# Transformer layer on eight cores: abs-sum tile loads alternate between the SyncE and GpSimd queues, some of these sums move into the V projection, and half of the layer-norm evacuations move to VectorE

## Chip, cores and metric

One Trainium2 chip, all eight cores. The time is the device time of one execution in microseconds (us), of the slowest core. Cores 0 to 3 are one die, 4 to 7 the other. Each core works alone on half of the query rows of one of four batch entries; the cores exchange nothing.

## What is computed

The layer is attention and a ternary-quantized FFN, each between layer norms and with a residual. Cut to what matters:

```python
def attn(x, Wq, Wk, Wv, Wo):              # x (4, 2048, 2048), 16 heads of 128
    scores = einsum('bthd,bshd->bhts', q, k) * tril(ones(T, T))
    attn = softmax(scores / T ** 0.5, axis=-1)
    return einsum('bhts,bshd->bthd', attn, v).reshape(B, T, D) @ Wo

def ternary_quant(w):                      # W_up, W_gate (8192, 2048), W_down (2048, 8192)
    scale = mean(abs(w)) + 1e-8
    q = clip(round(w / scale), -1, 1) * scale
    return w + stop_gradient(q - w)

x = x + layernorm(attn(layernorm(x), Wq, Wk, Wv, Wo))
x = x + layernorm(ffn(layernorm(x), W_up, W_gate, W_down))   # silu(up) * gate, down
```

The mask multiplies the scores (masked ones are 0, not minus infinity). What the change is about is `mean(abs(w))`: each core reads all of W_up, W_gate and W_down once, 192 MB in 192 tiles of 128 x 2048 f32 (1 MB each), and sums absolute values, before the FFN can start. The tiles are spread over the attention.

## The kernel before

The program is recorded engine by engine (`sec`, `Rec`) and replayed at one line, L1584 (`_replay`), so every instruction of the trace has this line: tiles tell them apart. Each engine runs its own list in order. `Buf.rd` and `Buf.wr` put the semaphore waits: a reader waits for the last writers of a buffer, a writer also for its readers, and so does a DMA that fills it. A DMA's wait is on the queue of the engine that issues it, so what stands behind it in that engine's list waits as well. SyncE (SP) and GpSimd (POOL) issue all DMAs.

The stages in order. (1) `emit_ln1`, 24 tiles of 128 rows: a load in two halves (`load_xtile`: first half from SP, second from POOL, which waits for the first), statistics (BN_STATS x4 and BN_AGGR) on DVE, rstd and the normalize on ACT, 16 transposes of 128x128 on PE in four groups of four, and one evacuation of 128x512 for each group, all on ACT (`emit_transposes`, default `evac="scalar"`). Three buffers rotate: xtA, xtB, xtC. Groups alternate between two PSUM tiles, psTr and psTr2, so group 2 needs group 0 evacuated. (2) The Q projection, 16 column blocks; the weights of a block are two halves, cast to bf16 on the way, from POOL, in two pairs of buffers (wqkA/wqkB, wqkC/wqkD). (3) Eight groups of two heads. `emit_group`: K of two heads, V of both (16 steps `st`, each 16 matmuls and one DVE cast into Vg), a matmul with U_b and a DVE cast into vsufT, the load of the next group's V weights (`load_wvg`: 16 DMAs on POOL into wvg, "arena_d<-WvR"), then `emit_head` twice. (4) Wo, residual and second layer norm, the FFN, the last layer norm: not touched.

`emit_head` has 16 chunks of shrinking width (1024 down to 128 columns). For a chunk: a score matmul on PE, two chunks ahead ("arena_c,arena_d"); a mask product on DVE in PSUM ("R<-R,arena_d"); the exponential on ACT (into stripA or stripB); on PE the denominator ("ones") and the product with V. At the end DVE adds the counts (den_f), ACT takes Ln and Exp of den_f, POOL stores it (den_spill), DVE casts the head's output (arena_b).

`emit_abs(n, which)` puts the next n abs-sums at the place where it is called. Each is a load of 1 MB into xtA or xtB by turns (both named arena_x in the trace), from SP, and one instruction: Down tiles ("DownR", "act") an Abs with an accumulated sum on ACT, Up and Gate tiles ("UpL", "GateL", by turns, "dve") a TENSOR_REDUCE on DVE into absP. A load waits until the sum before it in its buffer is done. The calls: two after each Q block and two after each K head (`which="any"`: Down tiles first), and one at every second chunk of each head (`which="dve"`), eight in a head. That is 64 Down tiles in the projections, 128 Up and Gate tiles in 16 heads. When "dve" has none left, it takes Down tiles while there are some. In the text the eight of a head are j0 to j7, xtA is A, xtB is B; heads count from 0, groups from 0, and group g has heads 2g and 2g+1.

Of the kernel before, what the change touches and what calls it, by code (L numbers as in the profile page):

```python
# [170 lines left out]
def build_program(p: Par, debug=False):  # L171
# [215 lines left out]
    def next_qreg():  # L387
        r = qkv8[qkv_rr[0] % 8]
        qkv_rr[0] += 1
        return r  # L390
# [7 lines left out]
    def qof(buf, tag):  # L398
        key = (id(buf), tag)
        if key not in dma_ctrs:  # L400
            dma_ctrs[key] = Counter(nc, f"q{tag}.{len(dma_ctrs)}", 16)
        return dma_ctrs[key]
# [27 lines left out]
    with nc.Block() as blk:  # L430

        def sec(engname):
            def runner(fn):
                fn(recs[engname], W[engname])
            return runner

        def dma_in(engname, dst, dst_ap, src_ap, deps=(), tag="i"):
            q = qof(dst, tag)
            @sec(engname)
            def _(e, w):  # L440
                w.wait(*deps)
                dst.wr(w)
                tok = q.inc(e.dma_start(out=dst_ap, in_=src_ap))
                dst.note_write(tok)
# [112 lines left out]
        def load_xtile(xt, src_ap):  # L557
            hD = p.D // 2
            dma_in("sync", xt, xt.ap[:, 0:hD], src_ap[:, 0:hD])
            dma_in("gpsimd", xt, xt.ap[:, hD:p.D], src_ap[:, hD:p.D], tag="i2")  # L560
# [48 lines left out]
        def emit_ln1():  # L609
            tiles = [("xs", t) for t in range(p.TT)] + [("xq", k) for k in range(p.QT)]  # L610
            n = len(tiles)

            def ld(i):
                srcname, ti = tiles[i]
                xt = xrot[i % 3][0]
                src = xs if srcname == "xs" else xq
                load_xtile(xt, src[ti * 128:(ti + 1) * 128, :])

            def st(i):
                xt, mv, rstd = xrot[i % 3]  # L620
                emit_ln_stats(xt, lambda xt=xt: xt.ap, mv, rstd, epsb)

            ld(0)
            st(0)
            if n > 1:
                ld(1)
            for i, (srcname, ti) in enumerate(tiles):
                xt, mv, rstd = xrot[i % 3]
                dstT = h_T if srcname == "xs" else hq_T
                dstW = p.T if srcname == "xs" else p.TQ  # L630
                t0 = ti * 128
                emit_normalize(xt, lambda xt=xt: xt.ap, mv, rstd, xt, xt.ap[:, :])
                if i + 1 < n:
                    st(i + 1)
                if i + 2 < n:
                    ld(i + 2)
                emit_transposes(xt, dstT, dstW, t0)

        emit_ln1()

        abs_state = {"next": 0, "next_act": 0, "next_dve": 0}
# [4 lines left out]
        def emit_abs(n, which="any"):  # L646
            for _ in range(n):
                if which in ("act", "any") and \
                        abs_state["next_act"] < len(abs_sched_act):
                    wi, ec = abs_sched_act[abs_state["next_act"]]  # L650
                    abs_state["next_act"] += 1
                elif abs_state["next_dve"] < len(abs_sched_dve):
                    wi, ec = abs_sched_dve[abs_state["next_dve"]]
                    abs_state["next_dve"] += 1
                elif abs_state["next_act"] < len(abs_sched_act):
                    wi, ec = abs_sched_act[abs_state["next_act"]]
                    abs_state["next_act"] += 1
                else:
                    return
                i = abs_state["next"]  # L660
                abs_state["next"] += 1
                src = (UpL, GateL, DownR)[wi]
                buf = xtA if i % 2 == 0 else xtB
                col = wi * 72 + ec
                dma_in("sync", buf, buf.ap[:, :], src[ec])
                if wi < 2:
                    @sec("vector")
                    def _(v2, w, buf=buf, col=col):
                        buf.rd(w)
                        tk = eV.inc(v2.reduce_sum(absP.ap[:, col:col + 1],  # L670
                                                  buf.ap[:, :], axis=AX.X,
                                                  apply_absolute_value=True))
                        buf.note_read(tk)
                        absP.note_write(tk)
                else:
                    @sec("scalar")
                    def _(s2, w, buf=buf, col=col):
                        buf.rd(w)
                        tk = eA.inc(s2.activation(buf.ap[:, :], buf.ap[:, :], AF.Abs,
                                                  accum_out=absP.ap[:, col:col + 1]))  # L680
                        buf.note_read(tk)
                        buf.note_write(tk)
                        absP.note_write(tk)
# [3 lines left out]
        def load_w_halves(dram, nb, pair, deps=()):  # L687
            dma_in("gpsimd", pair[0], pair[0].ap[:, :], dram[nb][:, 0:p.D // 2], deps)
            dma_in("gpsimd", pair[1], pair[1].ap[:, :], dram[nb][:, p.D // 2:p.D], deps)
# [45 lines left out]
        def kpair(ki):  # L735
            return wpairs[(p.DC + ki) % 2]
# [28 lines left out]
        def emit_group(gi):  # L765
            h0 = gi * p.NG
            for hh in range(p.NG):
                emit_proj_mms(h0 + hh, Kg, hh * p.T, h_T, p.T,
                              kpair(gi * p.NG + hh))
                emit_abs(2)  # L770
            for hh2 in range(p.NG):
                ki2 = (gi + 1) * p.NG + hh2
                if ki2 < nK:
                    load_w_halves(WkL, ki2, kpair(ki2))

            if gi == 0:
                load_wvg(0)

            for st in range(p.TT):
                reg = next_qreg()  # L780

                @sec("tensor")
                def _(t, w, st=st, reg=reg):
                    wvg.rd(w)
                    h_T.rd(w)
                    reg.wr(w)
                    hT = h_T.ap.rearrange("p (c t) -> p c t", c=p.DC)
                    ins = None
                    for dc in range(p.DC):
                        ins = t.matmul(reg.ap[:, 0:gw],  # L790
                                       hT[:, dc, st * 128:(st + 1) * 128],
                                       wvg.ap[:, dc * gw:(dc + 1) * gw],
                                       start=(dc == 0), stop=(dc == p.DC - 1))
                    tk = eP.inc(ins)
                    reg.note_write(tk)
                    wvg.note_read(tk)
                    h_T.note_read(tk)

                @sec("vector")
                def _(v, w, st=st, reg=reg):  # L800
                    reg.rd(w)
                    Vg.wr(w)
                    tk = eV.inc(v.tensor_copy(Vg.ap[:, st * gw:(st + 1) * gw],
                                              reg.ap[:, 0:gw]))
                    reg.note_read(tk)
                    Vg.note_write(tk)

            @sec("tensor")
            def _(t, w):
                U_b.rd(w)  # L810
                Vg.rd(w)
                psDen.wr(w)
                ins = None
                for c in range(p.TT):
                    ins = t.matmul(psDen.ap[0:p.TT, 0:gw],
                                   U_b.ap[:, c * p.TT:(c + 1) * p.TT],
                                   Vg.ap[:, c * gw:(c + 1) * gw],
                                   start=(c == 0), stop=(c == p.TT - 1),
                                   skip_group_check=True)
                tk = eP.inc(ins)  # L820
                psDen.note_write(tk)
                U_b.note_read(tk)
                Vg.note_read(tk)

            @sec("vector")
            def _(v, w):
                psDen.rd(w)
                vsufT.wr(w)
                tk = eV.inc(v.tensor_copy(vsufT.ap[:, :], psDen.ap[0:p.TT, 0:gw]))
                psDen.note_read(tk)  # L830
                vsufT.note_write(tk)

            if gi + 1 < p.NGRP:
                load_wvg(gi + 1)

            for hh in range(p.NG):
                emit_head(gi, hh)
# [3 lines left out]
        def emit_head(gi, hh):  # L841
# [56 lines left out]
            for ci, c in enumerate(chunks):  # L898
# [29 lines left out]
                if ci % 2 == 0:  # L928
                    emit_abs(1, which="dve")
# [705 lines left out]
```

How the kernel before makes its waits and increments, by code:

```python
    def inc(self, instr):  # L108
        instr.then_inc(self.sem, self.step)
        self.cnt += self.step
        return Tok(self.sem, self.cnt)
# [7 lines left out]
    def wait(self, *toks):  # L119
        for t in toks:
            if t is None:
                continue
            k = t.sem.num
            if self.hw.get(k, 0) < t.val:
                self.eng.wait_ge(t.sem, t.val)
                self.hw[k] = t.val
# [283 lines left out]
        def then_inc(self, sem, step):  # L410
            self.incs.append((sem, step))
            return self
# [4 lines left out]
        def wait_ge(self, sem, val):  # L417
            self.calls.append(("w", sem, val))
# [1152 lines left out]
        @sec("sync")  # L1571
        def _(sy, w):
            for ctr in dma_ctrs.values():
                if ctr.cnt:
                    sy.wait_ge(ctr.sem, ctr.cnt)
# [2 lines left out]
            def cb(eng):  # L1578
                for e in rec.calls:
                    if e[0] == "w":
                        eng.wait_ge(e[1], e[2])
                    else:
                        _, m, a, k, incs = e
                        ins = getattr(eng, m)(*a, **k)
                        for sem, step in incs:
                            ins.then_inc(sem, step)
```

## Time and profile before

| | |
|---|---|
| time, median of 2 runs | 3520.87 us (3366.25 and 3675.5) |
| the profiled execution, its own time | 3357.03 us |
| its span, slowest core (6 of 0 to 7) | 3355.5 us (cores: 3326.1 to 3355.5) |
| PE busy in the span | 2531.3 us, 75% |
| DVE, ACT, POOL busy | 1404.2 us (42%), 1128.4 us (34%), 314.1 us (9%) |
| DMA from SP's queue (q1) | 297.89 MB, 26.7% of the time of the 16 DMA engines |
| DMA from POOL's queue (q0) | 197.93 MB, 22.9% |

The span is the time from the first to the last instruction of a core; the run's time is 1.5 us more. Times in rows are us from the start of the span, unless marked ns. PE is the matmul array, PEld its weight load, DVE the vector engine, ACT the scalar engine. "R" is PSUM. "<-" ahead of a tile in brackets names what an idle time ended with. PEclk is the granted clock of PE as a share of full speed. The DMA share is the mean over 16 engines.

### The profile page before, as it was taken

To read this page: it belongs to the slowest core of one execution; us is meant where nothing else is said; L and a number is where in the kernel's file an instruction comes from. 1 tells how busy PE (TensorE), PEld (TensorE's weight loads), DVE (VectorE), ACT (ScalarE), POOL (GpSimd) and SP (SyncE) were. 2 spreads that over 40 slices of the span, in tenths; PEclk is the share of its full clock that TensorE was granted. 3 is DMA by queue.
4 is the path that set the end of the run, shared out by engine and by line. 5 is a ranking of instruction groups with operands and counts; after the bars stand their busy time and mean duration, and the time that the engine had idled before them with its cause. 6 is when DMAs were issued, how large, how long until landed. Compare 5 with 4: busy or idle time off the path is not lost.

```text
span 3355.5 us, 36902 instructions; the slowest of 8 cores (3326.1 to 3355.5 us)
## 1 busy us (share of the span) xinstructions
PE 2531.3 (75%) x11940; PEld 1250.9 (37%) x12132; DVE 1404.2 (42%) x1820; ACT 1128.4 (34%) x1269; POOL 314.1 (9%) x593
## 2 busy tenths in 40 slices
PE   3458678678577587676622999999999999999980
PEld 2333245245253353432211444444444444444430
DVE  3311143543534534530153535454444545453534
ACT  4643221312312222200024635344353525262602
POOL 1001111010110110001100101010010101010100
PEclk9869888788798897859965999999999999999995
DMA  4469854755755645512334635344353526261615
GB/s 132 134 185 258 216 142 140 252 134 162 218 146 189 199 139 203 172 24 40 44 97 142 226 103 171 130 145 157 120 182 96 191 86 199 82 209 67 208 37 163
DMA packets 136954, 498.18 MB, mean 148 GB/s; under 512 B 15728, under 2 KB 40304, under 8 KB 112192
## 3 DMA queue, kind: packets, MB, share of 16 engines
q1 hardware_dynamic: 54176, 297.89, 26.7%
q0 software_dynamic: 82592, 197.93, 22.9%
q8 instruction: 103, 1.69, 0.2%
q14 instruction: 83, 0.68, 0.1%
HBM read 512.46 MB, written 16.84 MB: 158 GB/s over the span
## 4 chain that ended last, share of the span: by engine, by line
PE 43%; DMA 21%; DVE 16%; issue 10%; ACT 9%; POOL 1%; DVEq 0%; ACTq 0%; POOLq 0%; SPq 0%
PE R L1584 43%; DMA arena_x<-GateL 8%; DVE arena_d L1584 4%; ACT qmC L1584 3%; DVE absP L1584 3%; DVE arena_b L1584 3%; ACT stripA L1584 2%; DVE stripB L1584 2%; ACT arena_d L1584 2%; DMA hbufA<-WoR 2%; DMA arena_x<-xs 2%; DVE stats L1584 2%; DMA wqkD<-WqL 2%; DMA hbufB<-WoR 1%; DMA arena_x<-UpL 1%
## 5 line engine op out<-in xcount | busy, mean ns | idle before, releaser
L1584 PE MATMUL R<-arena_c,arena_d 128*128 128x512 bf16 x4382 | 1016.7, 382 | 161.6 <-ACT stripB L1584 65.0
L1584 PEld LDWEIGHTS R<-arena_c,arena_d 128*128 128x128 bf16 x4480 | 436.2, 99 | 728.6 <-issue 246.5
L1584 PE MATMUL R<-arena_b,arena_d 128*128 128x512 bf16 x2007 | 447.9, 383 | 19.1 <-DVE arena_d L1584 17.0
L1584 ACT ACTIVATE arena_d<-arena_x,s_up 128x1024 bf16<-128x1024 f32 x128 | 146.5, 1144 | 607.5 <-DVE arena_d L1584 586.7
L1584 DVE TENSOR_REDUCE absP<-arena_x 128x1 f32<-128x2048 f32 x128 | 292.1, 2282 | 134.1 <-DMA arena_x<-UpL 80.7
L1584 PEld LDWEIGHTS R<-arena_b,arena_d 128*128 128x128 bf16 x2048 | 201.5, 99 | 265.5 <-issue 29.8
L1584 DVE CAST arena_d<-R 128x256 bf16<-128x256 f32 (+1 forms) x192 | 98.5, 513 | 376.0 <-PE R L1584 376.0
L1584 ACT ACTIVATE stripA<-R 128x256 bf16<-128x256 f32 (+5 forms) x128 | 86.2, 673 | 491.0 <-PE R L1584 341.3
L1584 PE MATMUL R<-arena_d,arena_a 128*128 128x256 bf16 x2048 | 227.4, 274 | 16.9 <-DMA arena_d<-WvR 16.9
L1584 DVE TENSOR_TENSOR down_acc<-down_acc,R 128x2048 f32<-128x2048 f32 x56 | 128.1, 2287 | 234.8 <-PE R L1584 234.8
L1584 DVE TENSOR_TENSOR arena_d<-arena_d,qmC 128x1024 bf16<-128x1024 bf16 x128 | 88.6, 692 | 315.1 <-ACT qmC L1584 315.1
L1584 PEld LDWEIGHTS R<-arena_d,arena_a 128*128 128x128 bf16 x2048 | 201.5, 98 | 43.4 <-issue 17.4
L1584 PE MATMUL R<-ident_b,arena_x 128*128 128x128 f32 x352 | 84.8, 421 | 161.0 <-ACT arena_x L1584 120.8
L1584 ACT ACTIVATE arena_x<-arena_x 128x2048 f32<-128x2048 f32 x64 | 122.0, 1906 | 154.7 <-DMA arena_x<-DownR 154.7
L1584 ACT ACTIVATE arena_d<-arena_x,s_gate 128x1024 bf16<-128x1024 f32 x128 | 146.0, 1140 | 57.2 <-DVE arena_d L1584 57.2
L1584 ACT ACTIVATE stripB<-R 128x128 bf16<-128x128 f32 (+5 forms) x128 | 79.7, 622 | 228.6 <-DVE R L1584 201.8
L1584 PE MATMUL R<-stripB,ones 128*128 128x512 bf16 (+1 forms) x192 | 60.2, 371 | 99.8 <-ACT stripB L1584 99.7
L1584 PEld LDWEIGHTS R<-ident_b,arena_x 128*128 128x128 f32 x352 | 67.2, 220 | 178.4 <-issue 178.3
L1584 POOL DMA_DIRECT2D arena_x<-GateL x128 | 68.7, 537 | 639.1 <-ACT stripA L1584 461.0
L1584 DVE TENSOR_TENSOR arena_d<-arena_d,stripA 128x1024 bf16<-128x1024 bf16 x128 | 87.8, 686 | 93.8 <-ACT stripA L1584 93.8
L1584 POOL DMA_DIRECT2D arena_x<-DownR x128 | 67.8, 530 | 582.5 <-DVE stripB L1584 574.9
L1584 PE MATMUL R<-stripA,ones 128*128 128x512 bf16 (+3 forms) x184 | 61.1, 393 | 79.0 <-ACT stripA L1584 79.0
(158 smaller groups left out, 2664.2 us busy)
## 6 DMA issues: line engine op xcount, KB each, us to landing
arena_x<-DownR SPq DMA_DIRECT2D x64, 1024.0 KB, 7.1
arena_x<-UpL SPq DMA_DIRECT2D x64, 1024.0 KB, 5.5
arena_x<-GateL SPq DMA_DIRECT2D x64, 1024.0 KB, 5.6
arena_x<-UpL SPq DMA_DIRECT2D x128, 512.0 KB, 5.1
arena_x<-GateL POOLq DMA_DIRECT2D x128, 512.0 KB, 4.6
arena_x<-DownR POOLq DMA_DIRECT2D x128, 512.0 KB, 6.1
arena_d<-WvR POOLq DMA_DIRECT2D x128, 64.0 KB, 4.9
arena_x<-xs SPq DMA_DIRECT2D x11, 512.0 KB, 4.4
```

The lines of the kernel that those rows point to most:

```text
L1584: ins = getattr(eng, m)(*a, **k)
```

## The change

Three edits. The transposes of the first layer norm are evacuated by DVE for groups 0 and 2 and by ACT for groups 1 and 3 (the branch `evac == "mixed"` was there). Every second abs tile, those of xtB, is loaded by POOL's queue, with a DMA semaphore of its own ("i3"). After every fourth step of a V stage one "dve" sum is put.

```diff
@@ emit_ln1
-                emit_transposes(xt, dstT, dstW, t0)
+                emit_transposes(xt, dstT, dstW, t0, evac="mixed")
@@ emit_abs
-                dma_in("sync", buf, buf.ap[:, :], src[ec])
+                dma_in("sync" if i % 2 == 0 else "gpsimd", buf,
+                       buf.ap[:, :], src[ec], tag="i" if i % 2 == 0 else "i3")
@@ emit_group, in the loop over st, behind the V cast
+                if st % 4 == 3:
+                    emit_abs(1, which="dve")
```

The number of tiles, and the bytes, stay: 192. The sums that V takes are missing at the end of the list: the last four "dve" calls of head 12 find no Up or Gate tile and take the last four Down tiles, on ACT; group 7's K stage and the heads 13, 14 and 15 have none.

POOL, groups 0 and 1, from the first wvg load. Before:

```order
L1584 DMA arena_d<-WvR 128x256 x32
L1584 DMA den_spill<-den_f 16x1x64 x2
L1584 DMA wqkA<-WkL 128x1024
L1584 DMA wqkB<-WkL 128x1024
L1584 DMA wqkC<-WkL 128x1024
L1584 DMA wqkD<-WkL 128x1024
L1584 DMA arena_d<-WvR 128x256 x16
```

Now:

```order
L1587 DMA arena_d<-WvR 128x256 x16
L1587 DMA arena_x<-GateL 128x2048 x2
L1587 DMA arena_d<-WvR 128x256 x16
L1587 DMA arena_x<-GateL 128x2048 x4
L1587 DMA den_spill<-den_f 16x1x64
L1587 DMA arena_x<-GateL 128x2048 x4
L1587 DMA den_spill<-den_f 16x1x64
L1587 DMA arena_x<-DownR 128x2048 x2
L1587 DMA wqkA<-WkL 128x1024
```

Two GateL loads belong to V's sums, four to each head. The first one of a head stands behind the 16 wvg DMAs or behind the other head's den_spill.

DVE, end of group 0's last head (its last sum), group 1's K and V, and the first chunks of head 2. Before:

```order
L1584 TENSOR_REDUCE absP<-arena_x 128x1
L1584 TENSOR_TENSOR R<-R,arena_d 128x128
L1584 TENSOR_TENSOR den_f<-R,counts_b 1x1024
L1584 CAST arena_b<-R 128x1024
L1584 CAST arena_d<-R 128x512 x8
L1584 CAST arena_d<-R 128x256 x16
L1584 CAST vsufT<-R 16x256
L1584 TENSOR_TENSOR R<-R,arena_d 128x128
L1584 TENSOR_REDUCE absP<-arena_x 128x1
```

The same stage in group 0, now (K casts, V casts in fours, vsufT, first chunk of head 0):

```order
L1587 CAST arena_d<-R 128x512 x8
L1587 CAST arena_d<-R 128x256 x4
L1587 TENSOR_REDUCE absP<-arena_x 128x1
L1587 CAST arena_d<-R 128x256 x4
L1587 TENSOR_REDUCE absP<-arena_x 128x1
L1587 CAST arena_d<-R 128x256 x4
L1587 TENSOR_REDUCE absP<-arena_x 128x1
L1587 CAST arena_d<-R 128x256 x4
L1587 TENSOR_REDUCE absP<-arena_x 128x1
L1587 CAST vsufT<-R 16x256
L1587 TENSOR_TENSOR R<-R,arena_d 128x128
L1587 TENSOR_REDUCE absP<-arena_x 128x1
```

V's 16 casts are cut into fours by a sum each; the head's own sums stay where they were.

DVE in the first layer norm, one tile. Before:

```order
L1584 BN_STATS stats<-xtC 128x6 x4
L1584 BN_AGGR mvC<-stats 128x2
L1584 TENSOR_SCALAR nmrC<-mvC,rstdC 128x1
L1584 BN_STATS stats<-arena_x 128x6 x4
L1584 BN_AGGR mvA<-stats 128x2
```

Now:

```order
L1587 BN_STATS stats<-xtC 128x6 x4
L1587 BN_AGGR mvC<-stats 128x2
L1587 CAST arena_a<-R 128x4x128 x2
L1587 TENSOR_SCALAR nmrC<-mvC,rstdC 128x1
L1587 BN_STATS stats<-arena_x 128x6 x4
```

The two casts are the evacuations of groups 0 and 2 of the tile before; they stand between the aggregate and the factor nmr that ACT's normalize reads.

## Rows read from the trace of the kernel before

**Rows 1.** windows: us; busy (instructions) of each engine; PEclk, DMA share, GB/s.
```profile
20.00:210.00 190.00, 92.46 (x384) 74.02 (x384) 70.30 (x144) 114.24 (x167) 11.10 (x21) 0.82 0.41 128
210.00:376.00 166.00, 124.90 (x513) 52.93 (x524) 24.02 (x32) 64.45 (x65) 19.14 (x36) 0.88 0.96 247
418.00:452.00 34.00, 32.56 (x272) 27.61 (x274) 6.79 (x16) 0.00 (x0) 2.29 (x5) 0.91 0.03 3
487.00:521.00 34.00, 18.76 (x76) 7.57 (x78) 23.90 (x26) 11.89 (x19) 0.51 (x1) 0.70 0.74 258
```

**Rows 2.** chain in order of time, start and us; Q projection, then heads 0 and 1.
```profile
247.78 0.47 issue
...
455.30 9.17 DMA arena_x<-UpL
...
495.92 5.53 DMA arena_x<-GateL
...
503.90 5.35 DMA arena_x<-GateL
```

**Rows 3.** timeline of DVE (start, us): V's end, heads 0 and 1.
```profile
449.34 0.42 DVE L1584 CAST arena_d<-R 128x256 bf16<-128x256 f32 x1 [1.32 <-PE R L1584]
...
452.95 2.28 DVE L1584 TENSOR_REDUCE absP<-arena_x 128x1 f32<-128x2048 f32 x1
...
484.11 2.29 DVE L1584 TENSOR_REDUCE absP<-arena_x 128x1 f32<-128x2048 f32 x1
...
487.62 1.21 DVE L1584 TENSOR_TENSOR den_f<-R,counts_b 1x1024 f32<-1x1024 f32 x1 [1.01 <-PE R L1584]
...
493.57 2.28 DVE L1584 TENSOR_REDUCE absP<-arena_x 128x1 f32<-128x2048 f32 x1
...
521.12 1.21 DVE L1584 TENSOR_TENSOR den_f<-R,counts_b 1x1024 f32<-1x1024 f32 x1 [1.08 <-PE R L1584]
```

**Rows 4.** timeline of POOL: wvg and den_spill of heads 0, 12, 13, 14, 15.
```profile
449.71 8.48 POOL L1584 DMA_DIRECT2D arena_d<-WvR  x16 [38.07 <-PE R L1584]
...
491.71 0.51 POOL L1584 DMA_DIRECT2D den_spill<-den_f  x1 [33.52 <-ACT den_f L1584]
...
1274.71 0.50 POOL L1584 DMA_DIRECT2D den_spill<-den_f  x1 [31.20 <-ACT den_f L1584]
...
1309.16 0.49 POOL L1584 DMA_DIRECT2D den_spill<-den_f  x1 [33.94 <-ACT den_f L1584]
...
1402.88 0.48 POOL L1584 DMA_DIRECT2D den_spill<-den_f  x1 [93.23 <-ACT den_f L1584]
...
1435.18 0.48 POOL L1584 DMA_DIRECT2D den_spill<-den_f  x1 [31.81 <-ACT den_f L1584]
```

**Rows 5.** DMA issues, KB each, median us to landing: 520-1440, 449-470, 40-200.
```profile
arena_x<-GateL SPq DMA_DIRECT2D x56, 1024.0 KB, 5.6
...
arena_x<-GateL SPq DMA_DIRECT2D x1, 1024.0 KB, 10.0
...
arena_x<-xq POOLq DMA_DIRECT2D x5, 512.0 KB, 3.9
```

**Rows 6.** timeline of ACT: exponentials of head 0 (two) and head 14 (first).
```profile
455.53 1.02 ACT L1584 ACTIVATE stripB<-R 128x1024 bf16<-128x1024 f32 x1 [1.37 <-DVE R L1584]
...
459.38 0.81 ACT L1584 ACTIVATE stripA<-R 128x768 bf16<-128x768 f32 x1 [0.17 <-PE R L1584]
...
1367.97 1.02 ACT L1584 ACTIVATE stripA<-R 128x1024 bf16<-128x1024 f32 x1 [46.28 <-PE R L1584]
```

**Rows 7.** timeline of the first layer norm, all engines.
```profile
80.40 0.26 DVE L1584 BATCH_NORM_AGGREGATE mvC<-stats 128x2 f32<-128x24 f32 x1
...
81.25 1.27 ACT L1584 ACTIVATE arena_a<-R 128x512 bf16<-128x512 f32 x2
...
84.00 0.33 SPq L1584 DMA_DIRECT2D arena_x<-xs  x1
```

**Rows 8.** groups of DVE by form, 376 to 1440: K's cast.
```profile
L1584 DVE CAST arena_d<-R 128x512 bf16<-128x512 f32 x64 | 44.2, 691 | 188.8 <-PE R L1584 188.8
```

## The prediction

> **What bounds the kernel now.** I read the stage table first. The FFN takes the last 1,485 us and the change does not touch it; what is touched lies before about 1,440 us. Four stretches matter [rows 1]. In the first (20 to 210, the layer norm of x and its transposes) nothing is full: DMA 0.41, ACT 114 of 190 us. It is a loop of latencies. In the second (210 to 376, the Q projection) the DMA engines are busy for 0.96 of the time, PE for 125 of 166 us: bandwidth. In the third (418 to 452, V of one group) PE is busy for 32.6 of 34 us, DVE for 6.8, and the DMA engines for 0.03. In the fourth (487 to 521, one attention head) no engine is full: PE 18.8, DVE 23.9, ACT 11.9 of 34 us.
>
> The chain of waits, in order of time, says what a head is made of: a sum of absolute values on DVE (absP), the load of the next 1 MB tile that it frees, 5.35 to 5.53 us, the next sum, and so on [rows 2]. There are two buffers, A (xtA) and B (xtB). A sum takes 2.28 us [rows 3], and a buffer comes round in 2.3 + 0.1 + 5.5 = 7.9 us, median landing 5.6 [rows 5]. A head has eight sums, j0 to j7 (even ones in A, odd ones in B), so four rounds, 31.6 us: den_f to den_f is 521.12 - 487.62 = 33.5 us [rows 3]. While DVE waits for a tile, the mask product behind it waits, then the exponential, then PE. So the loads of these sums set the length of every head.
>
> **Part 1, sums moved into V.** Each group gets four more DVE sums in its V stage. They come off the end: 128 DVE sums are used up after six groups of 20 and eight in group 6 (four in V, j0 to j3 of head 12). Head 12's j4 to j7 become ACT sums, taken from group 7's K stage, and heads 13, 14 and 15 have none. The cover in V is good: four sums are 9.2 us on a DVE that is idle for 27 of 34, and the DMA engines rest [rows 1]. The last one (B) sits between the last V cast and the vsufT cast, while PE does the U matmuls, so I cost it at nothing.
>
> A head without sums: the exponentials of the wide chunks follow at (459.38 - 455.53) / 3 = 1.28 us [rows 6]; as widths fall from 1024 to 128 I take 1.0 us for 15 gaps. Add 3.4 us from den_f to the next head's first exponential and 1.2 us at the end: 19.5 us. Bounds: 13 us if PE ran it back to back at full clock (18.8 us at a granted clock of 0.70 [rows 1], times 0.70), and 26 if these heads ran wholly at 1.2 GHz (18.8 times 1.4). Head 13 lies between the den_spill issues 1274.71 and 1309.16, 34.45 us: saves 15. Head 15 lasts 32.3: saves 13. Head 14 takes 34.9 us from its first exponential [rows 6] to the store [rows 4], and would take 15 + 1.2 + 4.1 = 20.3: saves 15. Together -43 us.
>
> **Part 2, B's loads on POOL.** This is the part that costs. Three effects.
>
> (a) The round of B. POOL starts 0.47 us after what it waited for [rows 2] and its issue lasts about 0.5 (0.53 for each of 16 in [rows 4]); SP starts at once. No 1 MB load from POOL is in this trace. Nearest rows: 3.9 us for 512 KB from POOL and 5.6 for 1 MB from SP [rows 5]. From below, B's round equals A's, 7.9; from above it has the whole 1.0 us and 0.4 more of landing, 9.3. I take 8.3: 5.5 us counted from POOL's start, as the halves of the layer norm land from either queue. B lags, A waits for it in DVE's order. That is 0.4 us in 3 rounds of 13 heads (head 12 counts, its ACT sums take turns in the same way), 16 us, contained in the next two sums.
> The Trainium skill (DMA: Bandwidth & Descriptors, "Anatomy of one DMA — SWDGE (gpsimd) path") fits such a DMA with about 2.0 us plus its bytes at 436 GB/s, 4.4 us for 1 MiB. No run here shows it yet; by it B's round would be 7.2 us, A would rule, and the sum would be some 16 us less.
>
> (b) First head of each group, counted from the start of the wvg issues at 449.71. Before, both tiles are in at its start: j0 at 452.95, j7 at 484.11 (+34.4), den_f at +37.9 [rows 3]. After, B is only freed by V's fourth sum, and on POOL its load stands behind 16 wvg issues, 8.5 us [rows 4], and behind their data. Before, the same work (wvg and two tiles) kept the engines busy until the later tile was in: issued after j1's sum at 457.8 (452.95, two sums of 2.28, a mask of 0.3), landing 10.0 us later [rows 5], so +18.2; the earlier one took 9.17 [rows 2]. So j1 starts at +18.3 instead of +5.8. Then j3, j5, j7 at +26.6, +34.9, +43.2, and den_f 3.5 us later: +46.7. That is +8.8 us for each of seven groups, 62 us. Bounds: j1 at +14.5 (issued at +9, no queue, 5.5 us) and +20.5.
>
> (c) Second head. B is free 1.2 us before den_f (484.11 + 2.3 = 486.4), and SP loads at once. POOL stands in front of den_spill, which it can issue only at 491.71 [rows 4], after both ACT passes over den_f. The GateL load behind it starts at 492.2, +4.6 from den_f, lands at +10.1, and j1 starts there instead of at 493.57, +5.95 [rows 3]. Then j7 at +35.0, den_f at +38.5 instead of +33.5: +5 us in six heads, 30 us. Behind a waiting load on POOL stand den_spill, whose reader comes after all heads, and the next group's wqk loads, which wait longer for PE. These cost nothing.
>
> In the Q projection B's loads stand between the weight loads. A stage at 0.96 DMA has the same bytes to move: 0, bounds -8 (PE no longer waits) and +26 (the next weights 1.6 us late in each of 16 steps of 10.4).
>
> **Part 3, half of the evacuations on DVE.** In the layer norm, SP loads a tile once PE has read its buffer. PE's second pair of transposes waits for ACT, which does rstd first, then evacuation 1, then 2 (81.25, 1.27 us for both), and SP goes at 84.00 [rows 7]. After, DVE evacuates the first right behind the aggregate (ends 80.66) in 0.69 us [rows 8], done at 81.35, while ACT starts the second at 81.25. PE's second pair starts 0.5 us sooner; this occurs once in two tiles, 12 times: -6 us. Bounds: -12, and +8 if nmr, now behind two casts, holds the normalize.
>
> **The sum.** +62 + 30 - 43 - 6 = +43 us. On the profiled execution's 3357.0 us (span 3355.5): 3400 us, +1.3%. The median of the two times shown, 3520.87, is a mean of 3366 and 3675; my base is the lower one, which the profiled execution nearly equals.
>
> **The rivals.**
> F: POOL's path costs nothing. B's round stays 7.9, den_spill holds nobody, and j1 of a first head is issued when V's last sum ends, +2.4, and lands in the 9.17 us of [rows 2], +11.6. A's j2 is then the one that lands at +18.3; j6 follows two rounds later at +34.1, j7 2.7 us on, den_f at +40.3, +2.4 over before. 17 for first heads, 0 for second: 17 - 43 - 6 = -32, 3325 us. For it: POOL's 512 KB land in 3.9 us. Against: POOL runs its queue in order, and den_spill's start is in the trace.
> S, the other side: two rings share the engines. If A's and B's bursts overlap, each lands later and B's round is 9.3, 1.0 us over my value in 39 rounds: +39, 3439 us, slower by 2.4%. It decides from 0.6 us a round. For it: tiles beside other traffic took 9.17 and 10.0 us. Against: a round of 8.3 us with two tiles has room, the DMA share in a head is 0.74 [rows 1].
> The Trainium skill (same page, "SWDGE vs HWDGE vs iDMA") says that the two kinds of DMA feed different queues inside each engine, which takes turns between them; in one queue the earlier tile goes first. That is the rule under S.
> Q: B's load on POOL holds the next weights in the Q projection, +26: 3426 us, about 2% slower.
> N: the sums are not gone but bunch up. If heads 13 to 15 took 27 us, PE's clock staying low in them, half the 43 us would go: +22, 3422 us.
>
> **How the numbers follow.** Forecast (3370 to 3425) 0.52, F 0.15, S 0.16, Q 0.09, N 0.04. There is 0.04 for more than 2% faster: F with the shortest empty heads and the best Q stage comes to 3357 - 32 - 19 - 8 = 3298, 1.8% faster, so it needs something I do not see. 2%, 67 us, is about what a measurement of this kernel can tell from no change. Slower by over 2%: S, half of Q and 0.05 of the forecast's upper tail, 0.26. Within 2%: 0.70. Faster: 0.04. The range reaches from F to past S: 3325 to 3450.
>
> **What would show it.** Right: first heads of some 50 us from the end of V to den_spill, second heads of 38 to 39, heads 13 to 15 below 21; in the chain GateL, not UpL, between sums; POOL waiting for den_f ahead of a GateL load; the layer norm ending near 204; V as long as before. Wrong: GateL from POOL landing above 6.2 us (S) or below 4.8; Q at more than 175 us; heads without sums above 24 us.

## The result, and the profile after

The changed kernel is slower by 2.3%: 1.0226 times before, 95% interval [1.0206, 1.0245]. The forecast was +1.3%, within 2%. The median of its twelve executions is 3629.96 us, but that holds executions in which one die or both ran at a lower clock; the ratio leaves them out, and the others took 3432.6 to 3437.8 us. The profiled execution took 3433.1 us and spans 3431.5, against 3355.5 before: +76 where I had forecast +43.

The windows of the profile after, on its slowest core (columns as in [rows 1]): V of group 0, its first head, its second head, and head 13, which has no sums.

```profile
412.00:446.00 34.00, 30.12 (x256) 26.01 (x256) 13.05 (x20) 0.00 (x0) 0.54 (x2) 0.89 0.42 129
448.00:495.00 47.00, 16.87 (x73) 7.39 (x73) 22.22 (x26) 9.75 (x16) 8.57 (x17) 0.70 0.69 200
495.00:538.00 43.00, 20.50 (x77) 8.04 (x76) 24.28 (x27) 11.85 (x18) 2.64 (x5) 0.66 0.54 196
1397.00:1412.00 15.00, 13.65 (x69) 6.15 (x70) 5.18 (x15) 8.11 (x14) 0.00 (x0) 0.93 0.01 2
```

V now has DMA and DVE work in it (0.42 and 13 us, against 0.03 and 6.8 in the third row of [rows 1]) and is no longer than it was. Head 13 is PE's: busy for 13.65 of 15 us at a granted clock of 0.93. A second head has the work of the fourth row of [rows 1] and takes 42 us instead of 34; the DMA share fell from 0.74 to 0.54, so the heads did not become longer for want of bandwidth.

The timeline of DVE after, heads 0 and 1: vsufT, the four sums of head 0 that work in B, its den_f, then head 1's first sum (497.73, in A), its first sum in B (507.67) and its den_f (start, us; in brackets the idle time before and its releaser):

```profile
448.42 0.41 DVE L1587 CAST vsufT<-R 16x256 bf16<-16x256 f32 x1 [0.18 <-PE R L1587]
...
464.41 2.29 DVE L1587 TENSOR_REDUCE absP<-arena_x 128x1 f32<-128x2048 f32 x1 [12.50 <-DMA arena_x<-GateL]
...
472.71 2.29 DVE L1587 TENSOR_REDUCE absP<-arena_x 128x1 f32<-128x2048 f32 x1 [1.14 <-DMA arena_x<-GateL]
...
482.14 2.29 DVE L1587 TENSOR_REDUCE absP<-arena_x 128x1 f32<-128x2048 f32 x1 [2.91 <-DMA arena_x<-GateL]
...
491.76 2.29 DVE L1587 TENSOR_REDUCE absP<-arena_x 128x1 f32<-128x2048 f32 x1 [4.15 <-DMA arena_x<-GateL]
...
495.26 1.21 DVE L1587 TENSOR_TENSOR den_f<-R,counts_b 1x1024 f32<-1x1024 f32 x1 [1.01 <-PE R L1587]
...
497.73 2.26 DVE L1587 TENSOR_REDUCE absP<-arena_x 128x1 f32<-128x2048 f32 x1
...
507.67 2.29 DVE L1587 TENSOR_REDUCE absP<-arena_x 128x1 f32<-128x2048 f32 x1 [6.37 <-DMA arena_x<-GateL]
...
537.65 1.21 DVE L1587 TENSOR_TENSOR den_f<-R,counts_b 1x1024 f32<-1x1024 f32 x1 [1.08 <-PE R L1587]
```

Set this beside [rows 3]: from j0 to j7 of the first head it was 484.11 - 452.95 = 31.2 us. Now j0 starts at 449.23 and j7 at 491.76, 42.5 us later, and DVE stands idle for 12.5 us in front of the first head's j1, and for 6.4 in front of the second's. The timeline of POOL says why, in both places:

```profile
445.99 8.46 POOL L1587 DMA_DIRECT2D arena_d<-WvR  x16 [10.62 <-PE R L1587]
454.31 0.68 POOL L1587 DMA_DIRECT2D arena_x<-GateL  x1
467.26 0.53 POOL L1587 DMA_DIRECT2D arena_x<-GateL  x1 [12.28 <-DVE R L1587]
...
499.34 0.51 POOL L1587 DMA_DIRECT2D den_spill<-den_f  x1 [13.82 <-ACT den_f L1587]
499.85 0.55 POOL L1587 DMA_DIRECT2D arena_x<-GateL  x1
...
1394.36 0.50 POOL L1587 DMA_DIRECT2D den_spill<-den_f  x1 [13.02 <-ACT den_f L1587]
1414.77 0.49 POOL L1587 DMA_DIRECT2D den_spill<-den_f  x1 [19.92 <-ACT den_f L1587]
```

The load of j1 is issued behind 16 wvg issues in the first head, and right behind den_spill in the second. The last two rows span head 13: 20.4 us, against 34.45 in [rows 4]. The chain of waits after, in order of time, its longest pieces:

```profile
454.31 10.01 DMA arena_x<-GateL
...
475.55 6.50 DMA arena_x<-GateL
...
484.99 6.68 DMA arena_x<-GateL
...
499.34 0.50 POOL den_spill L1587
499.85 7.73 DMA arena_x<-GateL
...
518.69 6.04 DMA arena_x<-GateL
...
527.66 6.32 DMA arena_x<-GateL
```

UpL, which was in the chain of before, is gone from it. The loads in it are GateL's from POOL, and at the start of the second head den_spill stands in it, ahead of such a load. Over the whole span the page of after gives, for 1 MB tiles, KB each and us to landing:

```profile
arena_x<-UpL SPq DMA_DIRECT2D x64, 1024.0 KB, 6.2
arena_x<-GateL POOLq DMA_DIRECT2D x64, 1024.0 KB, 6.1
```

**Where the 76 us come from.** I count a first head from the vsufT cast to its den_f and a second head from den_f to den_f, in the timelines of DVE of both kernels. The seven first heads with sums went from 35.0 us (mean) to 45.4: +73. The six second heads with sums went from 33.8 to 42.2: +50. Heads 13, 14 and 15 went from 34.4, 31.8 and 32.3 to 20.4, 15.7 and 20.4: -42. The vsufT cast of group 0 comes 3.7 us sooner (cores differ by more than that there, see part 3), and K and V of the last group are 2.9 us shorter. Together +74, and the last den_f indeed lies 74.7 us later (1431.14, then 1505.81).

### The profile page after: what moved, and what is told of

Same layout as the page of the kernel before. It is cut to its first block, busy times and chain, and to the rows that moved or that the text cites. A ratio compares the mean times of both kernels' runs of the same rounds, so it can differ in the third digit from the quotient of the medians.

```text
span 3431.5 us, 36940 instructions; the slowest of 8 cores (3417.7 to 3431.5 us)
## 1 busy us (share of the span) xinstructions
PE 2541.6 (74%) x11940; PEld 1255.1 (37%) x12132; DVE 1434.5 (42%) x1868; ACT 1101.9 (32%) x1221; POOL 366.0 (11%) x689
## 4 chain that ended last, share of the span: by engine, by line
PE 40%; DMA 20%; DVE 15%; issue 12%; ACT 10%; POOL 2%; DVEq 0%; ACTq 0%; POOLq 0%; SPq 0%
PE R L1587 40%; DMA arena_x<-GateL 8%; DVE arena_d L1587 4%; DMA arena_x<-DownR 4%; DVE arena_b L1587 4%; ACT qmC L1587 4%; DVE stripB L1587 2%; DMA hbufB<-WoR 2%; ACT arena_d L1587 2%; POOL arena_d L1587 2%; ACT stripA L1587 2%; DVE stats L1587 2%; DMA arena_x<-xs 1%; ACT arena_x L1587 1%; DMA hbufA<-WoR 1%
## 5 line engine op out<-in xcount | busy, mean ns | idle before, releaser
L1587 PEld LDWEIGHTS R<-arena_b,arena_d 128*128 128x128 bf16 x2048 | 201.7, 99 | 266.9 <-issue 31.8
L1587 POOL DMA_DIRECT2D arena_x<-GateL x192 | 103.9, 541 | 1095.8 <-ACT stripA L1587 462.7
L1587 POOL DMA_DIRECT2D arena_x<-DownR x160 | 86.0, 538 | 775.8 <-DVE stripB L1587 572.3
L1587 DVE SCALAR_TENSOR_TENSOR arena_d<-R,s_gate,silu_t 128x1024 bf16<-128x1024 f32 x64 | 81.8, 1278 | 69.6 <-PE R L1587 69.6
```

The lines of the kernel that those rows point to most:

```text
L1587: ins = getattr(eng, m)(*a, **k)
```

## The experiments

The table uses the same two measures, in us (means over the heads that have sums); the brackets hold the 95% interval of a ratio to the kernel before. The heads come from one profiled execution of each kernel. The last den_f also holds where the attention began, in which cores differ by some 10 us, so the heads are the finer measure.

| kernel | first head | second head | last den_f | ratio to before |
|---|---|---|---|---|
| before | 35.0 | 33.8 | 1431.1 | 1 |
| the change | 45.4 | 42.2 | 1505.8 | 1.0226 [1.0206, 1.0245] |
| e1, part 1 | 37.3 | 33.6 | 1394.5 | 0.9882 [0.9832, 0.9932] |
| e2, part 2 | 44.0 | 42.2 | 1564.5 | 1.0411 [1.0371, 1.0451] |
| e12, part 3 | 34.7 | 34.0 | 1427.1 | 0.9995 [0.9978, 1.0012] |
| e4, parts 1 and 3 | 36.6 | 34.2 | 1409.4 | 0.9891 [0.9842, 0.9939] |
| e5, den_spill from ACT | 44.8 | 37.4 | 1475.7 | 1.0127 [1.0006, 1.0248] |
| e6, wvg later | 41.9 | 41.9 | 1486.2 | 1.0119 [1.0035, 1.0203] |
| e7, both | 41.7 | 36.6 | 1453.3 | none |
| e9, both, all on SP | 35.4 | 34.0 | 1399.9 | 0.9904 [0.9872, 0.9936] |
| e10, both, all on POOL | 41.4 | 35.6 | 1441.6 | 1.0040 [1.0025, 1.0056] |
| e8, sums spread | 20.6 | 23.9 | 1267.2 | 0.9496 [0.9347, 0.9646] |
| e11, spread otherwise | 21.0 | 22.7 | 1302.7 | 0.9607 [0.9580, 0.9634] |

**One part at a time.** My theory: part 2 costs all of it, by the order of POOL's queue. The rival: the sums in V, or the casts in the layer norm, cost or give more than their terms.

e1, on the kernel before:

```diff
+                if st % 4 == 3:
+                    emit_abs(1, which="dve")
```

> Part 1 alone: V's sums, all loads on SP, evacuations as before. My theory (GpSimd's in-order queue and its slower loads cost, the moved sums gain): heads 13 to 15 take 20.4 us as in the changed kernel (-40 us), first heads of seven groups cost about 2.4 us each because only one tile is in when they begin (+17): 3335 us, 0.993 of before. Rival (the V sums are what lengthens the first heads, since V leaves B's buffer late): first heads stay near 50 us from V's end to the den_spill store, +55 to +70 in all, and the time is 3375 us or more.

Measured: faster by 1.2%, some 40 us. My term for the sums in V was -43. The two agree only as sums. Heads 13, 14 and 15 save 41 us, but each first head grows by 2.3 us (35.0 to 37.3), 16 us in seven: V's last sum leaves B to be filled while the wvg loads run. K and V of all groups, shorter by 5 us together, and a start that comes 5 us sooner make up for most of it.

e2, on the kernel before:

```diff
-                dma_in("sync", buf, buf.ap[:, :], src[ec])
+                dma_in("sync" if i % 2 == 0 else "gpsimd", buf,
+                       buf.ap[:, :], src[ec], tag="i" if i % 2 == 0 else "i3")
```

> Part 2 alone: B's tiles on GpSimd, no sums in V, evacuations as before. My theory: all 16 heads pay, with nothing saved at the end. Seven first heads +10 us (the load behind 16 wvg issues), eight second heads +8.4 (behind den_spill, and landings of 6.1 us): near 3490 us, 1.04 of before, and slower than the whole change. Rival (the V sums cost in the first heads): first heads stay at 42 us, only second heads cost, and the time is 3430 us or less.

Measured: slower by 4.1%, 138 us, more than the whole change loses. Part 2 alone costs 9.0 us in each of seven first heads and 8.4 in second heads; the last first head, head 14, with no wvg issues in front of its load, takes 32.0 us, as before (31.8). In the whole change part 1 empties heads 13, 14 and 15, which in e2 lose 8.8, 0.1 and 7.9 us. That is 17 us, and 138 - 40 - 17 = 81, near the 76 that the change costs. The parts nearly add up once this is counted.

e3 and e12 are the same edit, part 3 alone:

```diff
-                emit_transposes(xt, dstT, dstW, t0)
+                emit_transposes(xt, dstT, dstW, t0, evac="mixed")
```

> Part 3 alone: half of the layer-norm evacuations on VectorE. My theory: the layer norm ends 6 to 8 us sooner, PE's first Q matmul at about 209 us instead of 217, and the time is 3354 us, 0.998 of before. Rival (nmr behind the casts delays the normalize): no gain or a loss up to 8 us; the early start in the changed kernel would then come from core differences.

> Part 3 alone again, with more rounds. My forecast was -6 us. After the earlier runs, in which PE's first Q matmul starts at 204 to 226 us in kernels with either evacuation, I expect no difference: 1.000 of before, within 0.3 percent. If the forecast was right: 0.998 and a mean start over the cores that is 6 us sooner.

e3 gave no ratio; e12 did: 0.9995 [0.9978, 1.0012], no gain. Where the second eight transposes of the tile of [rows 7] start on PE, and what PE waited for, before:

```profile
81.98 1.94 PE L1584 MATMUL R<-ident_b,arena_x 128*128 128x128 f32 x8 [0.49 <-ACT arena_a L1584]
```

and the timeline of the same stage after:

```profile
79.90 0.20 ACT L1587 ACTIVATE rstdC<-rstdC 128x1 f32<-128x1 f32 x1
79.91 0.69 DVE L1587 CAST arena_a<-R 128x512 bf16<-128x512 f32 x1 [0.49 <-ACT rstdC L1587]
...
80.74 0.60 ACT L1587 ACTIVATE arena_a<-R 128x512 bf16<-128x512 f32 x1 [0.64 <-DVE arena_a L1587]
80.75 1.94 PE L1587 MATMUL R<-ident_b,arena_x 128*128 128x128 f32 x8 [0.16 <-DVE arena_a L1587]
...
82.69 0.20 DVE L1587 TENSOR_SCALAR nmrC<-mvC,rstdC 128x1 f32<-128x1 f32 x1
82.78 0.33 SPq L1587 DMA_DIRECT2D arena_x<-xs  x1
```

The evacuations start 0.8 us apart, one on each engine, in place of the pair on ACT in [rows 7], and PE waits for 0.16 us and not 0.49. That is a local gain of 0.3 us. From the start of the aggregate to SP's next load it is 3.6 us in both kernels (80.40 to 84.00, 79.15 to 82.78). The start of the first Q matmul over the eight cores, the end of this stage, is 213.0 us in the mean before, 212.8 after, 210.4 in e12, with cores from 204 to 219 among the three kernels: a gain of 0 to 3 us is below what one can read there.

e4 is parts 1 and 3 without part 2.

> Parts 1 and 3, only the queue edit undone. My theory: the parts add, -23 -8: 3330 us, 0.991 of before, so that the queue edit alone turns a gain of about 1 percent into a loss of 2.3. Rival (parts do not add, because the faster start meets a DMA-bound Q stage): the same time as part 1 alone.

Measured: 0.9891 [0.9842, 0.9939]. Taking part 2 away turns a loss of 2.3% into a gain of 1.1%.

**Which part of POOL's queue.** e5 is the whole change, with the store to den_spill issued by ACT; e6 is the whole change, with the wvg loads issued in the middle of the first head; e7 has both edits.

```diff
@@ e5: the section that stores to den_spill
-            @sec("gpsimd")
+            @sec("scalar")
@@ e6: emit_group, then emit_head behind the sums of a chunk
-            if gi + 1 < p.NGRP:
-                load_wvg(gi + 1)
+                if ci == 3 and hh == 0 and gi + 1 < p.NGRP:
+                    load_wvg(gi + 1)
```

> The whole change, with the store of den_f issued by ScalarE, so that GpSimd's queue no longer holds the second head's first GateL load until den_f is done. Theory Q1 (queue order): second heads fall from 42.2 to about 36 us (4.1 us of den_spill and the collision of that load with UpL), in six heads -35 us: near 3397 us, 1.011 of before. Rival Q2 (two rings share the engines, and that is what costs): the load is only issued earlier, all landings stay at 6.1 us, second heads stay above 39 us, time above 3410 us.

> The whole change, with the 16 wvg issues moved behind the second sum of the first head (chunk 3), so that they no longer stand in front of that head's first GateL load. Q1: first heads fall from 51.9 to about 45 us from V's end, seven times, -45 us: near 3390 us, 1.009. Rival Q2: wvg's data compete wherever they are, the 16 issues then stand in front of the next GateL load instead, first heads stay within 3 us of 51.9, time above 3415 us.

> Both moves together; B's tiles still come from GpSimd. Q1: nothing stands in front of B's loads but their own start (1.0 us more than SyncE): first heads about 45, second heads about 36 us, near 3350 us, 0.998. Q2: rounds stay at 9 us with landings of 6 us in both buffers, 3 rounds in 13 heads cost 40 us over the kernel with all loads on SyncE (3324 us), time 3370 us or more.

Measured: e5 takes 4.8 us from each second head and 0.6 from each first; e6 takes 3.5 from each first and 0.3 from each second; e7 has both effects; it gave no ratio, and its profiled execution spans 3374.2 us. So each wait is where the queue's order puts it, den_spill in second heads and wvg in first ones. But e6 gives back half of the 7 us a first head that I expected of it, and e7 (3375.7 us) ends where its rival had it (3370 or more): in e6 j1 starts 7.6 us from vsufT and not 16.0, and then j3 comes 14.1 us after it and not 8.1. In e5 j1 of a second head starts 6.6 us from den_f (mean of six), as before the change (6.0), not 12.4.

But e7 is still not e1: 41.7 against 37.3, and 36.6 against 33.6. Something of POOL's path remains when nothing stands ahead of its loads. e9 and e10 are e7 with all tile loads on one queue:

```diff
@@ e9
+                dma_in("sync", buf, buf.ap[:, :], src[ec])
@@ e10
+                dma_in("gpsimd", buf, buf.ap[:, :], src[ec], tag="i3")
```

> The kernel of e7_both (the store of den_f on ScalarE, wvg behind chunk 3), but with both buffers loaded by SyncE: the whole change without the queue edit and with both moves. It measures what is left of the queue edit when nothing stands in front of B's loads. If only SyncE's quicker start and landing are left, first heads 37 and second heads 33.5 us instead of e7_both's 41.7 and 36.6, near 3325 us, 0.989. Rival (the two moves themselves cost, for example by wvg's data in the middle of a head): first heads stay above 40 us.

> The same with both buffers loaded by GpSimd, so one ring again. R1 (the rest comes from two rings that share the engines): landings go back to 5.5 us, second heads 35 us or less, time at or below e7_both's 3375. R2 (the rest is GpSimd's later start, 1.0 us in each round): both buffers pay it, landings about 6 us, second heads 37 us or more, first heads 41 or more, time 3375 us or more.

e9 gives the whole loss back: 35.4 and 34.0 us, 0.9904 [0.9872, 0.9936], as fast as e1. e10, with all tiles in one ring (a ring is a queue of DMA work, one for POOL's and one for SP's), stays near e7: 41.4 against 41.7 us in first heads, 35.6 against 36.6 in second ones. In second heads one ring in place of two is thus worth 1.0 of the 2.6 us that lie between e7 and e9, and loading from POOL at all has the rest. First heads can't be split like this, for in e10 A's load of j2 comes to stand behind the 16 wvg issues as well (timelines of POOL and of DVE in e10):

```profile
461.64 0.53 POOL L1585 DMA_DIRECT2D arena_x<-UpL  x1
```

```profile
468.69 2.29 DVE L1585 TENSOR_REDUCE absP<-arena_x 128x1 f32<-128x2048 f32 x1 [8.30 <-DMA arena_x<-UpL]
```

Its buffer was free at 454.76. To see where the time goes, I took the time from each B sum to the next in the six full heads of each kind:

| kernel | j1 from vsufT | j1-j3, j3-j5, j5-j7, first | j1 from den_f | the same, second |
|---|---|---|---|---|
| before | 3.4 | 11.4, 8.1, 8.2 | 6.0 | 8.0, 8.0, 8.1 |
| the change | 16.0 | 8.1, 8.9, 9.0 | 12.4 | 8.1, 9.1, 9.0 |
| e7 | 7.6 | 13.6, 8.3, 8.3 | 6.7 | 8.8, 9.0, 8.6 |
| e9 | 6.8 | 9.5, 8.0, 7.9 | 6.6 | 8.3, 7.8, 7.8 |
| e10 | 6.3 | 13.5, 8.9, 9.5 | 6.6 | 8.5, 8.6, 8.4 |

(Before, the means are over eight heads.) Two residues stand out. With B on POOL, and e10 has this too, a round in a second head takes 8.5 to 8.8 us where SP's takes 8.0. And the round from j1 to j3 of a first head takes 13.6 on POOL and 9.5 on SP. In e7 that B load starts just after the wvg issues, 9.9 us behind the first of them:

```profile
454.10 8.48 POOL L1586 DMA_DIRECT2D arena_d<-WvR  x16
463.97 0.54 POOL L1586 DMA_DIRECT2D arena_x<-GateL  x1 [1.39 <-DVE R L1586]
```

and the sum that it feeds, from the timeline of DVE in e7:

```profile
474.92 2.29 DVE L1586 TENSOR_REDUCE absP<-arena_x 128x1 f32<-128x2048 f32 x1 [5.57 <-DMA arena_x<-GateL]
```

That is 10.95 us from issue to sum. In e9 the load of the same place comes from SP, with the same wvg data under way from POOL (chain of waits of e9, then its sum in the timeline of DVE):

```profile
473.25 7.55 DMA arena_x<-GateL
```

```profile
480.90 2.29 DVE L1585 TENSOR_REDUCE absP<-arena_x 128x1 f32<-128x2048 f32 x1 [1.84 <-DMA arena_x<-GateL]
```

7.65 us, 11.4 us behind the first wvg issue. In the seven groups these landings are 9.3 to 12.3 us in e7 and 6.3 to 7.6 in e9, and the round from j1 to j3 costs some 4 us more in e7. That is measured; its cause is not. A tile that must wait for the wvg data in the ring that both use would fit. But in e10 the same 16 issues stand in front of two tiles in POOL's ring, and they land in 7.0 to 7.6 and 8.9 to 9.5 us; and in the kernel before, SP's tile that is issued 8.1 to 8.6 us behind the first wvg issue takes 8.5 to 10.0. So what else is under way at that moment counts too (in e7 an UpL from SP, issued at 456.34, takes 10.23 us, in part beside it), and no run holds it fixed. The Trainium skill (DMA: Bandwidth & Descriptors, "SWDGE vs HWDGE vs iDMA") has the two kinds of DMA in different queues of each engine, which takes turns between them; no run here isolates that rule.

**Using what was learned.** What bounds a head is the number of sums in it, so e8 keeps every load on SP and the evacuations as before, and deals the sums out: one after each K head, six in V, four in a head instead of eight.

```diff
@@ emit_group, behind the sums of a K head
+                emit_abs(1, which="dve")
@@ emit_group, in V
+                if st in (1, 3, 6, 8, 11, 13):
+                    emit_abs(1, which="dve")
@@ emit_head
-                if ci % 2 == 0:
+                if ci % 4 == 0:
```

> All loads on SyncE, evacuations as before, and the sums spread evenly: one more VectorE sum at each K head, six in V (steps 1, 3, 6, 8, 11, 13), four in each head (every fourth chunk) instead of eight. If the round of load and sum (7.9 us) is what sets a head, a head with four sums has two rounds, 15.8 us, less than the 20.4 us of a head with none: heads of 22 to 26 us, K and V as long as before (55 us a group), 16 heads save about 12 us each: near 3170 us, 0.94 of before. Rival (DMA bandwidth shared by the cores is the limit, not the round): the bytes only move, K and V grow by what heads lose, and the time stays above 3300 us.

Measured: 0.9496 [0.9347, 0.9646], faster by 5%, the best kernel here; its profiled execution spans 3192.7 us. Heads take 20.6 and 23.9 us; K and V of a group take 62 to 68 instead of 62. DVE's waits between 500 and 1200 us in e8 (total, times, longest):

```profile
DVE R L1587 <- PE R L1587: 87.2, 70, 2.2
DVE absP L1587 <- DMA arena_x<-GateL: 34.6, 19, 4.5
...
DVE absP L1587 <- DMA arena_x<-UpL: 8.8, 9, 2.5
```

and the same stretch in the change:

```profile
DVE absP L1587 <- DMA arena_x<-GateL: 143.3, 36, 13.4
DVE R L1587 <- PE R L1587: 19.9, 14, 2.1
DVE absP L1587 <- DMA arena_x<-UpL: 10.4, 13, 1.6
```

In e8 the tiles are mostly in when DVE comes to them, and DVE waits for PE. The window 500 to 1200 of e8, columns as above:

```profile
500.00:1200.00 700.00, 581.37 (x3471) 339.26 (x3511) 379.08 (x488) 201.62 (x281) 70.25 (x133) 0.93 0.68 211
```

PE is busy for 581 of 700 us; the same line of before has 503, at a granted clock of 0.84.

e11 puts seven sums into V and seven into the two heads together:

```diff
-                if st in (1, 3, 6, 8, 11, 13):
+                if st in (1, 3, 5, 7, 9, 11, 13):
-                if ci % 4 == 0:
+                if ci in ((0, 4, 8, 12) if hh == 0 else (0, 5, 10)):
```

> The spread kernel e8_spread with one sum moved from each second head to V (seven in V, four in the first head, three in the second). If second heads of 23.8 us were still held by their fourth sum, they fall toward 21 us: 8 times 2.5, near 3175 us, 0.944. Rival (V is full with seven: a round of 7.9 us for two tiles is 28 us of V's 31): V and K grow from 64 to 67 us a group, and the time is the same as e8_spread or more, 3195 us.

Measured: 0.9607 [0.9580, 0.9634]. Second heads are 1.2 us shorter than in e8 (I had hoped for 2.5), but K and V of a group took 64.6 to 77.4 us, 69.4 in the mean, against 64.1 in e8. PE's waits between 530 and 700 us in e11 show the cause:

```profile
PE R L1587 <- DVE arena_d L1587: 25.4, 2, 14.7
```

(8.3 us in e8; from 500 to 1200 us it is 54.4 and 22.9.) V's matmuls wait for casts that stand on DVE behind a sum that waits for its tile. By these two kernels six sums in V is about the limit. e11's interval lies almost wholly within e8's, so which of the two is faster is not settled by the ratios; that both beat the kernel before is.

## Why the prediction was right and wrong

**Right: the view of the kernel.** A sum, the load of the next tile that it frees, the next sum: that this sets the length of a head is what every run shows, e8 most of all. That part 2 is the part that costs, too: e2 +4.1%, e1 -1.2%, e12 nothing.

**Right: part 1's saving.** The heads without sums take 20.4, 15.7 and 20.4 us where I took 19.5 for such a head, and save 42 us of my 43. Part 1 also has a cost, which I had put under POOL's effects: 2.3 of the 10.4 us that a first head loses are there in e1, with every load on SP. V's cover held: K and V of a group are 61 to 62 us in both kernels. Rival N, bunched work and a low clock, is false: the granted clock of head 13 is 0.93.

**Right: where j1 of the first head goes.** I said 18.3 us from the start of the wvg issues. It is 464.41 - 445.99 = 18.4, with a landing of 10.01 us, for which I had taken the 10.0 of [rows 5]. e6 shows that the wvg issues are the cause: without them in front j1 starts 8.4 us sooner. That the 10.0 of a tile from SP, beside another SP tile, came out as 10.01 for a tile from POOL is in part luck: over the seven first heads of the change this landing is 7.8 to 10.8 us.

**Too small: the round of B in effects (a) and (b).** I took 8.3 us a round. The change has 8.1, 8.9 and 9.0. Three rounds are 26.0 to 26.2 us and not 24.9, so 1.1 us is missing in a first head. The other 0.5 us there is the base: I had measured from one head of before, 35.5 us in the count used here, and the mean is 35.0. Together +10.4 and not +8.8 in seven heads, 11 us. The failure is in "5.5 us counted from POOL's start, as the halves of the layer norm land from either queue": halves of 512 KB at 3.9 us in another stage did not speak for 1 MB tiles with a second tile in flight. The GateL tiles of the later rounds land in 6.0 to 6.7 us in the chain above, and UpL from SP went from a median of 5.4 to 6.2 between 500 and 1200 us as well.

The estimate from the fit in the Trainium skill (DMA: Bandwidth & Descriptors, "Anatomy of one DMA — SWDGE (gpsimd) path") was 4.4 us for this load. The runs have 6.1 in the change, and 4.99 to 5.4 for the best single ones in e7: here the measurement decides, and the fixed part and rate of that fit are too kind when tiles follow one another.

**Too small: effect (c), the second head; this is the larger error.** I put j1 at +10.1 us from den_f. The queue's part was right: den_spill at 499.34, GateL issued 499.85, +4.6 us, which is what I had written. But it lands 7.73 us later, not 5.5, at +12.3. A is freed at 500.0 by the sum that starts at 497.73, so SP issues the next UpL at 500.07, 0.2 us after POOL issues GateL, and both tiles move at once. Before, the same two loads were issued at 486.48 and 492.43, 6 us apart. That is 2.3 us; with 1.3 of the rounds and -0.3 of the base a second head loses 8.4 and not 5 us, and six of them make 20 us of the error. I had noted that B's load would be late; I had not asked what it would then collide with. So the step that failed is the landing of 5.5 us for this tile: I had put its meeting with A's load at nothing. The runs bear the reading out. In the six second heads of the change the two are issued within 0.3 us of each other, and GateL lands in 7.3 to 8.0 us. In e5, whose POOL is not held by den_spill, the same load is issued 0.7 us ahead of den_f (1.0 in one head), at least 5.5 us ahead of UpL, and lands in 4.9 to 5.8. No run put only these two loads apart, with den_spill where it was.

**Part 3.** -6 us forecast, 0 to -3 measured, within what cores differ by. The tile shown saves 0.3 us and not my 0.5, and no saving can be told in the time of the whole.

**The sum.** 43 forecast; 11 from first heads, 20 from second heads, 2 from the start of the attention (3.7 us sooner for my 6), 1 from part 1 and -3 from the last group's K and V give the 74 measured. The time, 3433.1 us, lies within the whole range, 3325 to 3450, but above the 3370 to 3425 of the forecast itself: the direction and the places were right, and two terms of the sum too small.

**The rivals.** F, POOL's path costs nothing: false, since first and second heads lose 10 and 8 us. But its +2.4 us for a first head is what e1 shows without POOL's loads (+2.3). Q: false; from the first Q matmul to the first of K is 156 us before (217.7 to 373.8) and 157 after (209.2 to 366.2), so B's loads between the weights cost nothing there. S, overlapping bursts, had nearly the right time (3439); its sign, GateL landing above 6.2 us, is met by five of the six loads in the chain above but not by the median over the span, 6.1. The forecast's rounds were short by 0.4 of the 1.0 us that S gave. Two rings are only part of it: all loads in one ring (e10 against e7) give back 1.0 us in a second head, and first heads can't tell. The rest goes to POOL's start and issue, and to tiles in flight at the same time, whichever ring they are in. How these last two divide the 0.5 us a round that POOL costs over SP stays open.

## What to carry to other kernels

Before a load is moved to another engine's queue, write down what that engine has in front of it, instruction by instruction, and what the other instructions wait for: here a 1 MB load came to stand behind 16 small loads and behind a store that waits for two passes of another engine, and both waits went into the critical path. Then ask what the late load meets when it does start.

Where a stage is bounded by a side stream of loads and sums, the gain lies in spreading that stream over the stages that have room, in even portions, and not in a second queue for it: four sums from eight in a head gave 10 to 14 us a head, and the second queue alone cost 8 to 9 (e2).

## What the runs showed of the hardware

- Beside 16 small casting loads (64 KB each) a 1 MB tile lands late from either engine. From GpSimd, just behind their issues: 7.8 to 10.8 us in the change, 9.3 to 12.3 in e7, 7.0 to 7.6 in e10 (8.9 to 9.5 for the one behind it). From SyncE: 8.5 to 10.0 when issued 8.1 to 8.6 us behind the first of them (before), 6.3 to 7.6 when issued 11.4 to 12.4 us behind it (e9). What divides these is open.
- A 1 MB tile from GpSimd lands in 7.3 to 8.0 us when SyncE issues another of 1 MB within 0.3 us of it (second heads of the change), and in 4.9 to 5.8 when the other follows at least 5.5 us later (e5).
- GpSimd starts an issue 0.5 us after what releases it (a sum that ends at 475.00, the issue at 475.55) and is then busy for 0.53 us; SyncE starts 0.07 us after it (473.18 and 473.25 in e9). B's rounds in second heads are 8.5 to 8.8 us from GpSimd and 8.0 from SyncE, whether A shares its queue or not.
- A head of 16 chunks with four sums takes 21 to 24 us, a head without sums 16 to 20: four sums in a head are nearly hidden, eight are not (34 to 35).
